# Decoder feed-forward: the low halves of a body's first four hidden tiles, subtracted on VectorE between two row-maxima stages instead of on GpSimd

## What is computed

```python
for i in range(L):                                   # L = 4
    xn = layer_norm(x, ln1_w[i], ln1_b[i])
    x = x + mha(xn, mask, in_proj_w[i], in_proj_b[i], out_proj_w[i], out_proj_b[i])
    xn = layer_norm(x, ln2_w[i], ln2_b[i])
    h = jax.nn.gelu(xn @ ffn1_w[i].T + ffn1_b[i], approximate=False)
    x = x + (h @ ffn2_w[i].T + ffn2_b[i])
```

## Time and profile before

| what | before |
|---|---|
| median of 3 runs | 3541.78 us (3535.92 to 3551.64) |
| the profiled execution, its own time | 3547.18 us |
| its span, first to last instruction | 3545.4 us |
| PE busy | 3327.9 us, 94% |
| DVE busy | 2603.5 us, 73% |
| ACT busy | 2353.1 us, 66% |
| POOL busy | 1419.8 us, 40% |
| mean granted TensorE clock | 0.970 of full |

### The profile page before, as it was taken

The page is one execution under the profiler, slowest core; times in us unless marked ns, Lnnn a source line. Parts: engine busy times, 40 slices in busy tenths (PEclk is TensorE's granted clock), DMA queues, the critical chain, the costliest instruction groups (busy, mean ns, idle before and its releaser), DMA issues. The chain is left out here.

```text
span 3545.4 us, 90224 instructions
## 1 busy us (share of the span) xinstructions
PE 3327.9 (94%) x36704; PEld 2322.9 (66%) x36704; DVE 2603.5 (73%) x5236; ACT 2353.1 (66%) x3538; POOL 1419.8 (40%) x1308
## 2 busy tenths in 40 slices
PE   5899999999999999999994988799999999999998
PEld 3677676776767767677762655466666666666665
DVE  4666667666676766767646888898888888888867
ACT  4677777777777777777743676566666666666665
POOL 1233232332323233232324552564454444444475
PEclk8999999999999999999996899899999999999999
DMA  3100111101111011110002122100000000000001
GB/s 121 42 29 29 41 50 37 38 29 41 42 44 36 31 41 41 45 35 31 30 1 86 57 64 75 63 13 26 1 26 26 1 26 1 26 1 26 1 13 37
DMA packets 102764, 124.56 MB, mean 35 GB/s; under 512 B 17648, under 2 KB 90608, under 8 KB 100080
## 3 DMA queue, kind: packets, MB, share of 16 engines
q1 hardware_dynamic: 102352, 118.78, 10.2%
HBM read 50.13 MB, written 8.39 MB: 17 GB/s over the span
## 5 line engine op out<-in xcount | busy, mean ns | idle before, releaser
L2708 POOL TENSOR_TENSOR e_hT<-e_h,e_hT 128x512 f16<-128x512 f32 x512 | 614.1, 1201 | 603.6 <-ACT e_hT L2457 580.6
L1017 DVE TENSOR_REDUCE mx<-maxima_pair 128x4 f16<-128x1024 f32 (+1 forms) x384 | 470.1, 1224 | 234.7 <-PE maxima_pair L504 232.2
L2451 ACT ACTIVATE e_h<-e_h,e_b 128x512 f32<-128x512 f32 x512 | 365.3, 714 | 417.4 <-DVE e_h L2537 417.3
L93 PE MATMUL bank<-xT,w_half 128*128 128x512 f16 x2304 | 535.2, 383 | 3.9 <-DVE xT L960 3.9
L815 ACT ACTIVATE PR<-scores_pair 128x1024 f32<-128x1024 f32 x384 | 392.6, 1022 | 127.5 <-PE scores_pair L521 119.0
L1123 POOL TENSOR_TENSOR QK<-qk,QK 128x512 f16<-128x512 f32 x128 | 148.2, 1158 | 629.4 <-ACT qk L744 434.2
L2395 PE MATMUL bank<-VS,e_hT 128*128 128x256 f16 x3072 | 389.5, 273 | 5.2 <-DVE VS L2500 4.1
L2395 PE MATMUL bank<-e_w,e_hT 128*128 128x256 f16 x3072 | 388.7, 273 | 4.6 <-POOL e_hT L2708 4.3
L93 PEld LDWEIGHTS bank<-xT,w_half 128*128 128x128 f16 x2304 | 216.4, 98 | 246.1 <-issue 12.5
L2395 PEld LDWEIGHTS bank<-VS,e_hT 128*128 128x128 f16 x3072 | 300.7, 98 | 112.1 <-DVE VS L2500 4.6
L2395 PEld LDWEIGHTS bank<-e_w,e_hT 128*128 128x128 f16 x3072 | 300.6, 98 | 109.9 <-POOL e_hT L2708 6.5
(11 more groups left out here) (221 smaller groups left out, 7011.1 us busy)
## 6 DMA issues: line engine op xcount, KB each, us to landing
QS<-QK SPq DMA_DIRECT2D x240, 128.0 KB, 2.1
KS<-QK SPq DMA_DIRECT2D x192, 128.0 KB, 2.1
PR<-in_expert_weights SPq DMA_DIRECT2D x16, 1024.0 KB, 4.9
stage<-in_weights SPq DMA_DIRECT2D x48, 256.0 KB, 3.5
c_x<-in_x SPq DMA_DIRECT2D x8, 512.0 KB, 4.4
xT_f<-c_xT SPq DMA_DIRECT2D x8, 512.0 KB, 3.7
stage<-xT_f SPq DMA_DIRECT2D x4, 1024.0 KB, 5.5
out<-stage SPq DMA_DIRECT2D x8, 512.0 KB, 3.5
```

The costliest lines, as they stand in the source:

```text
L93: last = pe.matmul(out, stat(a, k), mov(b, k), start=(k == 0 and n == 0), stop=(k == tiles - 1 and n == 2))
L1017: dve.tensor_reduce(out, src, AX.X, ALU.max, negate=True).then_inc(mx_in.sem, 1)
L2451: act.activation(h32[r % 2][:, j, :], h32[r % 2][:, j, :], ACT.Gelu, bias=b1[:, e, m:m + 1], scale=1.0 / WS)\
L2708: pool.tensor_tensor(hT[r % 2][1][:, f, part], h32[r % 2][:, j, :], hT[r % 2][0][:, f, part], ALU.subtract)\
```

## The change

GpSimd no longer makes low halves in the decoder. Its four subtractions of a body, tiles 0 to 3, go to VectorE: two right behind `maxima(n+1, 1, 0)` and two right behind `maxima(n+1, 1, 1)`. Tiles 4 to 7 stay where they were, behind the norm. Both semaphores `h_l` are now raised by VectorE; the wait for `Y_ps` moves from tile 4 to tile 0. Buffers, TensorE's and ScalarE's orders, and the DMAs are as before. (One empty line goes too, so that later lines of the decoder carry a number one lower.)

```diff
@@ -925,7 +924,7 @@
 
     @block.vector
     def _(dve):
-        for s in (w_lo, qb_ready, ln1_steps, z1, xl1, mx_in, rd_in, on_in, ol, xo, ln2_steps, z2, xl2, y_x, h_l[1]):
+        for s in (w_lo, qb_ready, ln1_steps, z1, xl1, mx_in, rd_in, on_in, ol, xo, ln2_steps, z2, xl2, y_x, *h_l):
             dve.sem_inc(s.sem, s.credit())
 
         def weights(l, part):
@@ -938,10 +937,10 @@
         def hidden_low(n, m):
             dve.wait_ge(h_h.sem, h_h.after(n - 1, m + 1))
             dve.wait_ge(h_f.sem, h_f.after(n - 1, m + 1))
-            if m == KF // 2:
+            if m == 0:
                 dve.wait_ge(Y_ps.sem, Y_ps.after(n - 2))
             dve.tensor_tensor(hT[1][:, m, :], h32[:, m % NH32, :], hT[0][:, m, :], ALU.subtract)\
-               .then_inc(h_l[1].sem, 1)
+               .then_inc(h_l[m // NH32].sem, 1)
 
         def query_bias(l):
             dve.wait_ge(ahead_in.sem, ahead_in.after(l))
@@ -1090,7 +1089,15 @@
                 weights(l, "f2")
             if ahead:
                 maxima(n + 1, 1, 0)
+            if back:
+                hidden_low(n, 0)
+                hidden_low(n, 1)
+            if ahead:
                 maxima(n + 1, 1, 1)
+            if back:
+                hidden_low(n, 2)
+                hidden_low(n, 3)
+            if ahead:
                 maxima(n + 1, 1, 2)
                 if not (kind is STEADY and isinstance(n, int) and n + 2 >= L * NG):
                     if kind is PRE:
@@ -1105,7 +1112,7 @@
 
     @block.gpsimd
     def _(pool):
-        for s in (v_in, qk_l, h_l[0], xb1, xb2):
+        for s in (v_in, qk_l, xb1, xb2):
             pool.sem_inc(s.sem, s.credit())
 
         def values(n, k):
@@ -1122,13 +1129,6 @@
                 pool.wait_ge(heads_in[1].sem, heads_in[1].after(n - 1))
             pool.tensor_tensor(QK[1][:, m, :], qk32[:, m % 2, :], QK[0][:, m, :], ALU.subtract).then_inc(qk_l.sem, 1)
 
-        def hidden_low(n, m):
-            pool.wait_ge(h_h.sem, h_h.after(n - 1, m + 1))
-            pool.wait_ge(h_f.sem, h_f.after(n - 1, m + 1))
-            if m == 0:
-                pool.wait_ge(Y_ps.sem, Y_ps.after(n - 2))
-            pool.tensor_tensor(hT[1][:, m, :], h32[:, m % NH32, :], hT[0][:, m, :], ALU.subtract).then_inc(h_l[0].sem, 1)
-
         def add_row(g, row, done):
             for t in range(TT):
                 last = pool.tensor_tensor(x[:, bass.ds(g * TT + t, 1), :], x[:, bass.ds(g * TT + t, 1), :],
@@ -1157,11 +1157,6 @@
                 add_row(g, 1, xb1)
             if ahead:
                 query_key_low(n + 1, 3)
-            if back:
-                hidden_low(n, 0)
-                hidden_low(n, 1)
-                hidden_low(n, 2)
-                hidden_low(n, 3)
 
         all_bodies(pool, body)
```

## The result

| what | before | after |
|---|---|---|
| median | 3539.43 us (3535.92 to 3551.64, 4 runs) | 3581.04 us (3575.92 to 3582.68, 4 runs) |
| ratio of the runs | | 1.0116, 95% interval 1.0100 to 1.0133 |
| the profiled execution, its own time | 3547.18 us | 3581.46 us |
| its span | 3545.4 us | 3579.6 us |
| DVE busy | 2603.5 us | 2682.1 us |

The runs of the kernel before are the three of the table further up and a fourth. The change makes the kernel 1.2% slower, 41.6 us by the medians. 3578 us was forecast, in a range of 3560 to 3592.

A forecast was written before the change was run, and what follows sets the result against it. TensorE runs through and VectorE has idle time, but none from stage (1,2) to the seam. 29 bodies at 1.24 us plus 0.6 give 36.6, rounded to 36: 1.0% more, 3578 us, range 3560 to 3592.

The forecast's parts named there:

- The removal is worth nothing: On GpSimd: dropping four subtractions a body of 1156 ns each gains 0, since nobody waited for them.
- First stall: TensorE ahead of stage (1,2) of row scores: idle 0.60 us a body because maxima (1,1) end late.
- Lateness of VectorE at stage (1,2): Stage (1,2) of maxima starts 1.33 us late, behind the subtraction that needs the Gelu of tile 3.
- The seam absorbs 0.09: Between two bodies, at TensorE's OS 3: 0.09 us of VectorE's lateness is absorbed, 1.24 us reaches TensorE.
- The second stall: TensorE at OS 3, waiting for late `outputs` 0: the other 0.64 us of the 1.24 a body.
- The sum: Whole program: bodies 1 to 29 lose 1.24 us each, body 30 loses 0.6; 36.6 us, rounded down to 36.
- Hidden: Rival, chance 0.08: VectorE's 3.97 us of idle time hold the 2.41 us of work; time stays at 3542.
- First stall only: Rival, chance 0.07: only TensorE's 0.60 us ahead of stage (1,2) counts, 18 us in all; 3560.
- Clock: Rival, chance 0.04: TensorE's two stalls lower its clock to 1.2 GHz once a body, 51 us more; 3629.
- Faster: Rival, chance 0.03: tile 4's Gelu gets its slot sooner as VectorE frees it, up to 17 us gained; 3525.

The follow-up runs named there:

- seam_to_pool: The change, but with the subtractions of tiles 4 to 7 on GpSimd instead of VectorE: 3596.51 us, ratio 1.0158 to the kernel before.
- first_pair: Kernel before, with only tiles 0 and 1 moved to VectorE, behind stage (1,0) of maxima; tiles 2 and 3 stay on GpSimd: 3561.93 us, ratio 1.0062.
- one_stage_later: The change, but each pair of subtractions stands behind the next stage of maxima, (1,1) and (1,2): 3569.36 us, ratio 1.0085 to the kernel before.
- second_pair: Kernel before, with only tiles 2 and 3 moved to VectorE, behind stage (1,1) of maxima: 3580.25 us, ratio 1.0112.
- work_only: Kernel before, plus four extra VectorE subtractions a body on constant data at the change's two places; GpSimd keeps its four: 3543.03 us, ratio 1.0007.
- wait_only: Kernel before, but VectorE waits for the Gelus of tiles 1 and 3 ahead of stages (1,1) and (1,2), taking over no subtraction: 3563.01 us, ratio 1.0071.

## Why the prediction was right

**The removal is worth nothing.** Held: GpSimd's busy time fell by 150 us (148 forecast), VectorE's rose by 79 (80 forecast), and no view shows a gain from either. The period of ordinary bodies went up by what VectorE's lateness gives, with nothing left over to attribute. The reason given for GpSimd not slowing VectorE was too narrow, though: it looked at the maxima alone, and the second norm of the kernel before has an operation that GpSimd stretches to 1.16 us (under seam_to_pool). It happens that the four moved subtractions didn't lie beside such an operation. The rule of the Trainium skill (GPSIMD Engine Reference, section 4.1) has GpSimd about twice as slow; the durations are 1156 ns against 691, a factor of 1.7, and they decided nothing here.

**First stall, 0.60 us.** Held: 0.60 us idle, the start 0.66 later. The 0.06 are the handover again, 0.11 in place of 0.05 (`gelu` 1 ends at 655.36 + 0.69 = 656.05, the subtraction starts at 656.16). first_pair has this stall alone and costs 22 us.

**Lateness of VectorE at stage (1,2), 1.33 us.** The mechanism held, and the term was a little small: 1.39. I took 0.60 from the start of one subtraction to the start of what follows, from four that run back to back. Behind a wait the same spacing is 656.77 - 656.16 = 0.61, and the handover was 0.1 in place of 0.05 (`gelu` 3 ends at 658.07 + 0.68 = 658.75 by ScalarE's timeline, and the subtraction starts at 658.85).

**The seam absorbs 0.09, the rest reaches TensorE.** Held, and it was the step on which most hung. Body 20 of before had given it for a lateness of 0.33; the experiments repeat it at others: 1.20 costs 1.10 a body (one_stage_later), 1.39 costs 1.29 (the change) or 1.30 (second_pair, with no first stall at all). The second stall is the remainder of one lateness and no cost of its own.

**The sum.** 29 x 1.29 + 0.66 = 38.1 us for the ordinary accounting against 36 forecast; the traces have 40.5 or 39.2 up to the end of the decoder. The rest lies in the bodies around new weights, and there it is the clock: body 17 takes 56.30 us in place of 53.32, 1.7 more than the 1.29, and stands at 0.50 where before it stood at 1.00 (1036.20 above):

```profile
1058.10:1061.30 3.20, 3.20 (x9) 1.21 (x8) 2.08 (x3) 1.93 (x4) 0.00 (x0) 0.50 0.00 0
```

Body 14 takes 2.75 more. second_pair, with the same ordinary period, doesn't have either and is 36.5 us later than before at the end of the decoder. That the medians came within 3 us of the forecast is therefore luck in part; the period, 55.92 against 55.8 to 55.9 forecast, is the firmer test.

**The rivals.** *Hidden* fell twice over: work_only shows that the work is indeed hidden, wait_only that the waits alone cost 23 us. *First stall only* fell with first_pair and second_pair: the first stall alone costs 22 us, and the cost is 40 without it. (It would have needed a slack of 1.33 - 0.60 = 0.73 us at the seam, not 0.8.) *Clock*: two windows of the kernel after, over bodies with two stalls each, have the full clock:

```profile
160.00:430.00 270.00, 265.33 (x3790) 188.60 (x3789) 188.94 (x425) 198.24 (x282) 60.97 (x68) 1.00 0.10 32
660.00:890.00 230.00, 225.88 (x3206) 160.56 (x3206) 163.52 (x377) 169.94 (x242) 50.82 (x56) 1.00 0.09 31
```

so stalls of 0.6 and 0.5 us did not lower it. Where the clock stood lower than before, in bodies 14 and 17, it had fallen behind the idle times of 3.5 and 2.3 us for weights. *Faster* fell with the result; no run tried it apart.

## What to carry to other kernels

An engine that works its queue in order has idle time only until the moment its next input is ready: before you put work there, compare when its inputs are ready with when the next thing in the queue is wanted, and add up the lateness to the first place that has no slack. Share of busy time did not decide here: four subtractions in the idle time cost 0, waiting for two tiles' Gelus with no work at all 23 us, and two subtractions in the wrong place 40. Look also at what an engine stands beside, not only behind: a move from VectorE to GpSimd took away 2.4 us and cost 3.1 on small operations of the norm. And where the part of the program that a change doesn't touch varies by several us from one execution to the next, compare the touched part in the traces as well as the medians.

## What the runs showed that I had not expected

- Beside a subtraction on GpSimd, 0.17 us operations on VectorE took up to 1.16 us, and two subtractions that take 1.28 us together took 2.32 (work_only). In body 10 of the kernel before, GpSimd's four subtractions of low halves lie beside maxima, which read PSUM and keep their 1.23 us, and beside the first operations of the norm (BN_STATS), four of which take 1.39 us there and 1.40 in the change, without GpSimd beside them.
- The handover from ScalarE to VectorE has no one price: 0.03 us for the `oT` subtraction of the earlier trace rows, 0.10 for a low half that waits for two Gelus (after: 658.75 to 658.85), and 0.15 behind the bare waits of wait_only (708.83 to 708.98).
